# The four score products of an attention section take their banks together

## The chip, the cores and the metric

The kernel runs on one core of one Trainium2 chip. The metric is the device time of one execution in microseconds (us), the median of three runs. The core has five engines with a program each: TensorE (PE in the profile, with its weight loads as PEld), VectorE (DVE), ScalarE (ACT), GpSimd (POOL) and SyncE (SP). They meet at semaphores only.

## What is computed

A decoder of four layers with twelve sections (three kinds of attention, a delta rule, a state space section, dense and expert feed-forward sections) over 32 sequences of 128 tokens with 128 features. The change lies in the attention sections with 16 heads of 8 features, of which there are four. This is the one without a mask, cut to what matters:

```python
def _L0_xattn_ref(q, k, v, Wq, Wk, Wv, Wo):
    N_HEADS = 16
    query = split_heads(q @ Wq.T)
    key_ = split_heads(k @ Wk.T)
    value = split_heads(v @ Wv.T)
    scores = jnp.einsum('bhqd,bhkd->bhqk', query, key_) / jnp.sqrt(...)
    attn_probs = jax.nn.softmax(scores, axis=-1)
    attn_out = jnp.einsum('bhqk,bhkd->bhqd', attn_probs, value)
    return attn_out.transpose(0, 2, 1, 3).reshape(B, S, D_MODEL) @ Wo.T

x = x + _L0_xattn_ref(_layernorm(x, axis=-1), ctx_1024, ctx_1024, ...)
```

The other three (`L1_attn`, `L2_attn`, `L2_cross`) add a causal or a given mask to the scores before the softmax.

## The kernel before

Two streams (`STREAMS = 2`, called 0 and 1) of `G = 2` sequences each run interleaved. A round takes both through all twelve sections, and there are eight rounds; stream 1 starts six sections on, so that different sections of the two streams meet, and a first part brings stream 1 to that place. Inside a round each engine runs its own fixed list: the program of a stream is a Python generator for each engine, cut at its `yield`s, and the strings `TURNS` say for each engine which stream's next piece comes. Nothing reorders the lists afterwards. A "w" in the string of PE is a small product that nobody reads (`warm`, L2354).

Partial sums lie in eight PSUM banks. Two (`ACC`, one for each stream) are kept for accumulations, the other six form a ring that both streams share (`class Psum`). `open` gives the next bank of the ring and, on PE, emits a wait until the reader of the bank's last contents has given it back (semaphore `bank{b}_emptied`, incremented by `give`). `close` marks it filled; `take` is the reader's wait for that.

`attention16` is the code of the four sections. In it, for each sequence s of the two:

- `products(s, "S", ...)` (called by `scores`) makes the scores of 16 heads as four products, j = 0 to 3 (L728). Each contracts 32 rows (partitions 32j to 32j+31, so that each lies in its own quarter of TensorE's rows), has 512 columns in float32, and writes one bank. A float32 product is two MATMUL instructions in the profile, so four products are eight.
- With a mask, four more products (L698 causal, L701 given) add it, and only these close the banks. Without one (`L0_cross`, named x0) each product closes its own bank.
- DVE takes the negated maximum of each bank (`maxima`, L874) and gives the bank back; four short steps (L878 to L881) split the maxima into parts (`mparts`), which PE transposes (L747).
- `products(s, "T", ...)` makes the same scores transposed, again four products at L728. The subtraction of the maxima (L762) is added on PE, which closes the banks, and ACT takes the exponentials (L838, called from the piece behind L830). `values` (L778) multiplies with the values, `divide` (L886, L887) on DVE normalises.

The order of pieces on PE is: S of sequence 0, S of sequence 1, transposition and T of sequence 0, values and T of sequence 1, and so on. In x0 of stream 1 the other stream is in `L3_mamba`: on ACT L1622 to L1640, on DVE L1683 to L1713, on PE L1543 to L1577. Its preparation ends on DVE with L1687, which waits for ACT's L1628, and with L1692 to L1696, which wait for ACT's L1640; then 32 steps with a scan (L1707) each follow.

Of the kernel before, what the change touches and what calls it, by code (L numbers as in the profile page):

```python
# [25 lines left out]
B, L, D = 32, 128, 128  # L26
# [5 lines left out]
NJ, NI = 4, 4  # L32
# [286 lines left out]
def row_tiles(ap):  # L319

    return ap.rearrange("p (s f) -> p s f", f=128)
# [10 lines left out]
def build(nc, dram, out):  # L332
    with ExitStack() as st:
# [87 lines left out]
        def col(s):  # L421
            return slice(s * L, (s + 1) * L)
# [81 lines left out]
        def stream(u):  # L504
# [20 lines left out]
            def program(P, part):  # L525
# [149 lines left out]
                def attention16(nm, w, src=None, bias=False, bias_out=False, rope=False, mask=None):  # L675
# [29 lines left out]
                    def pe_f(pe):  # L705
# [6 lines left out]
                        for name, wn, s_ in todo:  # L712
                            t = P.open(pe, f"{nm}.{name}")
                            P.close(pe.matmul(t, W[w + wn][:], s_[:], start=True, stop=True), f"{nm}.{name}")
                        yield
                        t = P.open(pe, nm + ".v")
                        if bias:
                            bias_row(pe, t, W[w + "bv"][:])
                        for s in range(G):
                            last = pe.matmul(t[:, col(s)], src_ap[:, col(s)], W[w + "Wv"][:], start=not bias, stop=True,  # L720
                                             skip_group_check=True)
                        P.close(last, nm + ".v")

                        def products(s, letter, lhs, rhs):
                            for j in range(NJ):
                                r = slice(32 * j, 32 * j + 32)
                                t = P.open(pe, f"{nm}.{letter}{s}{j}", width=NI * L)
                                last = pe.matmul(row_tiles(t), lhs[r, col(s)], rhs[r, s], start=True,  # L728
                                                 stop=letter == "S" and mask is None, skip_group_check=True)
                                if letter == "S" and mask is None:  # L730
                                    P.close(last, f"{nm}.{letter}{s}{j}")

                        def scores(s):
                            yield
                            if s == 0 and not rope:
                                P.wait_given(pe, nm + ".q")
                            pe.wait_ge(ev(f"{u}.kz"), base["kz"] + s + 1)
                            products(s, "S", qk[0], kz)
                            if mask:
                                for j in range(NJ):  # L740
                                    P.close(masking(pe, P.bank(f"{nm}.S{s}{j}"), False, s), f"{nm}.S{s}{j}")

                        def turned(s):
                            yield
                            pe.wait_ge(ev(f"{u}.mparts"), base["mparts"] + s + 1)
                            t = P.open(pe, f"{nm}.mT{s}")
                            P.close(pe.transpose(t.bitcast(BF16)[:, 0:L], mparts[:, s, :], ident_bf[:]), f"{nm}.mT{s}")  # L747
                            yield
                            if s == 0:
                                pe.wait_ge(ev(f"{u}.qz"), base["qz"] + 1)  # L750
                            products(s, "T", qk[1], qz)
                            for j in range(NJ):
                                if j % 2 == 0 and j:
                                    yield
                                if mask:
                                    masking(pe, P.bank(f"{nm}.T{s}{j}"), True, s)
                                if j == 0:
                                    P.wait_given(pe, f"{nm}.mT{s}")
                                t = P.bank(f"{nm}.T{s}{j}")
                                for i in range(NI):  # L760
                                    a = NI * j + i
                                    last = pe.matmul(t[:, i * L:(i + 1) * L],  # L762
                                                     sel_part[:, a:a + 1].broadcast_to([128, 128]), mT[:, col(s)],
                                                     start=False, stop=i == NI - 1, skip_group_check=True)
                                P.close(last, f"{nm}.T{s}{j}")
# [26 lines left out]
                        t = P.open(pe, nm + ".y", ACC)  # L792
                        if bias_out:
                            bias_row(pe, t, W[w + "bo"][:])
                        for s in range(G):
                            yield
                            P.wait_given(pe, f"{nm}.O{s}")
                            last = pe.matmul(t[:, col(s)], oT[:, col(s)], W[w + "Wo"][:], start=not bias_out, stop=True,
                                             skip_group_check=True)
# [1625 lines left out]
        P = Psum(banks, filled, emptied)  # L2425
# [144 lines left out]
```

## Time and profile before

| what | value |
|---|---|
| median of three runs | 4992.15 us (4987.52 to 4992.7) |
| the profiled execution, its own time | 4994.97 us |
| its span, first to last instruction | 4993.3 us |
| mean granted clock of TensorE | 0.86 of full speed |
| PE / PEld / DVE / ACT / POOL busy | 82% / 57% / 65% / 41% / 13% |

The page of the profile gives busy time by engine, the span in 40 slices, and the costliest groups of instructions by line. The trace behind it can be asked for a stretch: the timeline lists instructions in order of time with the idle time of their engine before them and what released it, the list of waits sums such idle times by pairs, and the table of stretches gives busy time and granted clock (the PEclk column; 1.00 is 2.4 GHz, 0.50 is 1.2 GHz). The span without what lies around it is 1.7 us under the execution's own time.

### The profile page before, as it was taken

The numbers are of one execution on the slowest core, as the hardware profiler recorded it, in microseconds if no ns is written. First come the engines' busy times: TensorE is split into PE (matmuls) and PEld (weight loads), VectorE is DVE, ScalarE is ACT, GpSimd is POOL, SyncE is SP. The second block draws the span as 40 slices with busy tenths as digits, with TensorE's granted clock in tenths as the row PEclk, the third lists the DMA queues.
The fourth block names the chain that finished last, engine by engine and source line by source line (L and its number), as shares of the span: only waits on it lengthen the run. The fifth ranks groups of instructions, "written<-read, shape, count | busy, mean of one in ns | idle before, by whom it ended". The sixth has DMA issues, their size and how long they took to land. (4 is left out here: it accounts for less than half of the span.)

```text
span 4993.3 us, 97444 instructions
## 1 busy us (share of the span) xinstructions
PE 4078.1 (82%) x38655; PEld 2833.0 (57%) x38655; DVE 3236.5 (65%) x8464; ACT 2059.6 (41%) x4978; POOL 671.0 (13%) x1030
## 2 busy tenths in 40 slices
PE   2688888888888898888888888888888888888883
PEld 1455565656556566656556565555656565555652
DVE  3467767576766757676775767677675767677661
ACT  1245353534435353444435353443535344353530
POOL 1010201102010111101020110102011010102002
PEclk9689889798888889888888988898898988798897
DMA  4000000000000000000000000000000000000013
GB/s 125 1 2 1 7 1 7 1 3 5 1 7 1 6 2 7 2 1 7 1 7 1 6 2 6 2 1 7 1 7 1 4 4 1 7 1 6 2 33 89
DMA packets 70922, 46.81 MB, mean 9 GB/s; under 512 B 13095, under 2 KB 67488, under 8 KB 70226
## 3 DMA queue, kind: packets, MB, share of 16 engines
q1 hardware_dynamic: 65024, 33.82, 2.4%
q8 instruction: 322, 5.28, 0.4%
q0 software_dynamic: 2048, 3.85, 0.3%
q10 hardware_dynamic: 3378, 2.64, 0.2%
q14 instruction: 150, 1.23, 0.1%
HBM read 30.14 MB, written 10.50 MB: 8 GB/s over the span
## 5 line engine op out<-in xcount | busy, mean ns | idle before, releaser
L728 PE MATMUL banks<-scratch 32*128 32x512 f32 x2112 | 584.3, 764 | 74.8 <-ACT scratch L1635 36.2
L838 ACT ACTIVATE scratch<-banks 128x512 f32<-128x512 f32 x528 | 276.5, 600 | 254.6 <-PE banks L762 254.4
L301 ACT ACT_TABLE_LOAD x293 | 375.9, 1283 | 10.1 <-PE banks L1055 4.9
L874 DVE TENSOR_REDUCE scratch<-banks 128x4 f32<-128x512 f32 x528 | 330.0, 683 | 59.5 <-PE banks L728 36.1
L728 PEld LDWEIGHTS banks<-scratch 32*128 32x128 f32 x2112 | 205.3, 214 | 255.6 <-issue 84.8
L1650 ACT ACTIVATE scratch<-scratch,ssm_A 128x256 f32<-128x256 f32 x512 | 229.5, 500 | 264.5 <-DVE scratch L1707 251.9
L1562 PE MATMUL banks<-scratch,w_ident 128*128 128x256 f32 x1024 | 282.6, 399 | 57.0 <-DVE scratch L1713 56.9
L1707 DVE TENSOR_TENSOR_SCAN scratch<-scratch 128x512 f32<-128x512 f32 x256 | 313.2, 1224 | 12.6 <-ACT scratch L1650 5.2
L1846 PE MATMUL banks<-scratch 32*32 32x32 f32 (+1 forms) x11152 | 251.8, 206 | 48.8 <-issue 28.1
L1846 PEld LDWEIGHTS banks<-scratch 32*32 32x32 f32 (+1 forms) x11152 | 219.6, 119 | 101.9 <-issue 73.0
L1192 PE MATMUL banks<-experts,scratch 128*128 128x128 f32 x1792 | 261.3, 294 | 9.1 <-ACT scratch L1228 6.3
L1192 PEld LDWEIGHTS banks<-experts,scratch 128*128 128x128 f32 x1792 | 248.9, 207 | 30.2 <-issue 10.8
L1228 ACT ACTIVATE scratch<-banks,w_e_b 128x256 f32<-128x256 f32 x448 | 191.0, 472 | 174.7 <-PE banks L1184 173.2
L553 POOL TENSOR_TENSOR 1_rstd<-1_var,minus_half 128x2 f32<-128x2 f32 x102 | 75.5, 740 | 1354.8 <-DVE 1_var L571 1283.8
L1562 PEld LDWEIGHTS banks<-scratch,w_ident 128*128 128x128 f32 x1024 | 180.9, 195 | 105.9 <-DVE scratch L1713 87.8
L553 POOL TENSOR_TENSOR 0_rstd<-0_var,minus_half 128x2 f32<-128x2 f32 x96 | 67.1, 699 | 1190.5 <-DVE 0_var L571 1015.5
L886 DVE RECIPROCAL scratch<-banks 128x128 f32<-128x128 f32 x132 | 126.1, 955 | 151.9 <-PE banks L778 151.2
L778 PE MATMUL banks<-scratch 128*32 128x128 f32 x4224 | 220.5, 281 | 1.3 <-ACT scratch L838 1.3
L762 PEld LDWEIGHTS banks<-scratch,sel_part_bf 128*128 128x128 bf16 x2112 | 166.0, 105 | 95.6 <-issue 41.6
L2354 PE MATMUL banks<-ident_bf 128*128 128x256 bf16 x1128 | 175.6, 299 | 53.2 <-ACT scratch L824 21.7
L1701 DVE TENSOR_TENSOR scratch<-scratch,banks 128x512 f32<-128x512 f32 x256 | 174.5, 682 | 67.4 <-PE banks L1577 67.4
L778 PE MATMUL banks<-scratch,w_slots 128*32 128x128 f32 x4224 | 215.3, 276 | 0.0
(515 smaller groups left out, 8932.7 us busy)
## 6 DMA issues: line engine op xcount, KB each, us to landing
experts<-in_e_W SPq DMA_DIRECT2D x16, 256.0 KB, 5.4
w_e_W<-in_e_W SPq DMA_DIRECT2D x3, 704.0 KB
expert_in<-scratch SPq DMA_DIRECT2D x1, 2048.0 KB, 14.2
scratch<-expert_in SPq DMA_DIRECT2D x8, 256.0 KB, 4.6
expert_out<-scratch SPq DMA_DIRECT2D x8, 256.0 KB, 2.3
scratch<-residual SPq DMA_DIRECT2D x8, 256.0 KB
out<-scratch SPq DMA_DIRECT2D x8, 256.0 KB
experts<-in_e_w SPq DMA_DIRECT2D x1, 1792.0 KB, 7.8
```

What stands on the lines that cost most here:

```text
L301: act.preload_act_table_set(name)
L728: last = pe.matmul(row_tiles(t), lhs[r, col(s)], rhs[r, s], start=True, stop=letter == "S" and mask is None, skip_group_check=True)
L778: last = pe.matmul(t[32 * i:32 * i + 32, k * L:(k + 1) * L], W["slots"][:, 32 * j:32 * j + 32] if k else vslot[:, s, j, i, :], pT[:, s % 2 ...
L838: P.give(act.activation(pT[:, s % 2, j, :], t, ACT.Exp), f"{nm}.T{s}{j}")
L874: P.give(dve.tensor_reduce(negm[:, s, NI * j:NI * j + NI], row_tiles(t), X, ALU.max, negate=True), f"{nm}.S{s}{j}")
L1192: last = pe.matmul(t[:, col(s)], hid[:, e % RING, c, col(s)], w2[:, 2 * e + c, :], start=c == 0, stop=c == 1, skip_group_check=True)
L1228: P.give(act.activation(hid[:, e % RING, c, :], t, ACT.Gelu, bias=W["e2_b1"][:, 2 * e + c:2 * e + c + 1]), f"{nm}.u{e}.{c}")
L1562: last = pe.matmul(total[:, c * N:(c + 1) * N], ident[:], yc[:, k % RING, j, :], start=False, stop=n == DS - 2 and j == 1, skip_group_chec ...
L1650: ins = act.activation(decay[:, k % RING, j, :], dstart[:, c, :], ACT.Exp, scale=ssm_A[:, c, n + j:n + j + 1])
L1707: dve.tensor_tensor_scan(*flat, 0.0, ALU.mult, ALU.add).then_inc(ev(nm + ".state"), 1)
L1846: last = pe.matmul(t[dst, h * width:(h + 1) * width], lhs(h), rhs(h), start=True, stop=True, skip_group_check=True)
L2354: pe.matmul(banks[:, bank, 0:N].rearrange("p (s f) -> p s f", s=G), ident_bf[:], spread(ident_bf[:], G), start=True, stop=True, skip_group ...
```

## The change

The four banks of a group of four products are opened before the first product, in the same ring order. The waits that `open` emits therefore all stand in front of the product j = 0, and the products j = 1 to 3 wait for nothing. This holds for both letters, S and T, in all four sections. The turns, the banks of each name, the number of waits and the instructions of every engine stay as they are.

```diff
                         def products(s, letter, lhs, rhs):
+                            t = [P.open(pe, f"{nm}.{letter}{s}{j}", width=NI * L) for j in range(NJ)]
                             for j in range(NJ):
                                 r = slice(32 * j, 32 * j + 32)
-                                t = P.open(pe, f"{nm}.{letter}{s}{j}", width=NI * L)
-                                last = pe.matmul(row_tiles(t), lhs[r, col(s)], rhs[r, s], start=True,
+                                last = pe.matmul(row_tiles(t[j]), lhs[r, col(s)], rhs[r, s], start=True,
                                                  stop=letter == "S" and mask is None, skip_group_check=True)
```

On PE, in x0 of stream 1 within a round (S of sequence 0, S of sequence 1, the transposition, T of sequence 0), with each row's semaphores; `1.kz`, `1.qz` and `1.mparts` are operands that DVE and ACT prepare:

```order
-L728 MATMUL banks<-scratch 128x512 [waits bank5_emptied,1.kz,bank2_emptied]
-L728 MATMUL banks<-scratch 128x512 [waits bank0_emptied]
-L728 MATMUL banks<-scratch 128x512 [waits bank1_emptied]
-L728 MATMUL banks<-scratch 128x512 [waits bank2_emptied]
-L728 MATMUL banks<-scratch 128x512 [waits bank3_emptied,1.kz]
-L728 MATMUL banks<-scratch 128x512 [waits bank4_emptied]
-L728 MATMUL banks<-scratch 128x512 [waits bank5_emptied]
-L728 MATMUL banks<-scratch 128x512 [waits bank0_emptied]
+L728 MATMUL banks<-scratch 128x512 [waits bank0_emptied,bank1_emptied,bank5_emptied,bank2_emptied,1.kz]
+L728 MATMUL banks<-scratch 128x512 x3
+L728 MATMUL banks<-scratch 128x512 [waits bank5_emptied,bank4_emptied,bank0_emptied,bank3_emptied,1.kz]
+L728 MATMUL banks<-scratch 128x512 x3
```

No product has moved; the waits for banks 0 and 1 now stand ahead of the product into bank 5.

On DVE at the same place, the rows are the same before and after (`bank5_filled` says that the product j = 0 of sequence 0 has ended, `0s3.high` and `0s3.soft` come from ACT for the other stream):

```order
L874 TENSOR_REDUCE scratch<-banks 128x4 [waits bank5_filled,1.ones]
L1687 TENSOR_TENSOR scratch<-scratch 32x1024 [waits 0s3.high]
L874 TENSOR_REDUCE scratch<-banks 128x4 [waits bank0_filled,0s3.parts]
L874 TENSOR_REDUCE scratch<-banks 128x4 [waits bank1_filled]
L874 TENSOR_REDUCE scratch<-banks 128x4 [waits bank2_filled]
L878 CAST scratch<-scratch 128x16 [waits bank2_emptied]
L879 TENSOR_TENSOR scratch<-scratch 128x16 [waits dve_steps]
L880 CAST scratch<-scratch 128x16 [waits dve_steps]
L881 TENSOR_TENSOR scratch<-scratch 128x16 [waits dve_steps]
L1692 TENSOR_TENSOR scratch<-scratch 128x512 [waits 0s3.soft]
```

Nothing moved here; the first maximum stands ahead of L1687 in DVE's list.

## Rows read from the trace of the kernel before

**Rows 1.** The page, part 5: busy us, mean ns, idle before and releaser.

```profile
L728 PE MATMUL banks<-scratch 32*128 32x512 f32 x2112 | 584.3, 764 | 74.8 <-ACT scratch L1635 36.2
```

**Rows 2.** Timeline of PE, masked section: start us, length us, instructions [idle before <-releaser].

```profile
1622.00 1.14 PE L728 MATMUL banks<-scratch 32*128 32x512 f32 x8
1623.07 1.04 PE L698 MATMUL banks<-causal_bf,ident_bf 128*128 128x512 bf16 x4
1624.04 3.00 PE L728 MATMUL banks<-scratch 32*128 32x512 f32 x8
1626.97 1.04 PE L698 MATMUL banks<-causal_bf,ident_bf 128*128 128x512 bf16 x4
```

**Rows 3.** The same view at the half clock, a group that waits for no bank.

```profile
2031.84 2.09 PE L728 MATMUL banks<-scratch 32*128 32x512 f32 x8 [0.73 <-issue]
```

**Rows 4.** Who released L728's weight loads: us, times.

```profile
  DVE scratch L874: 85.8, 142
  ACT scratch L1635: 71.1, 40
```

**Rows 5.** Timeline of all engines, x0 of stream 1 in round 3.

```profile
1843.72 1.09 PE L728 MATMUL banks<-scratch 32*128 32x512 f32 x2 [0.84 <-issue]
1844.92 0.69 DVE L874 TENSOR_REDUCE scratch<-banks 128x4 f32<-128x512 f32 x1 [0.70 <-PE banks L728]
1846.97 1.22 DVE L1687 TENSOR_TENSOR scratch<-scratch 32x1024 bf16<-32x1024 f32 x1 [1.36 <-ACT scratch L1628]
1847.34 0.47 ACT L1635 ACTIVATE scratch<-banks,w_s_dt_b 128x256 f32<-128x256 f32 x1
1847.86 5.00 PE L728 MATMUL banks<-scratch 32*128 32x512 f32 x14 [3.05 <-ACT scratch L1635]
1848.05 0.48 ACT L1635 ACTIVATE scratch<-banks,w_s_dt_b 128x256 f32<-128x256 f32 x1
1848.58 0.62 PEld L728 LDWEIGHTS banks<-scratch 32*128 32x128 f32 x7 [0.23 <-ACT scratch L1635]
1850.04 1.94 DVE L874 TENSOR_REDUCE scratch<-banks 128x4 f32<-128x512 f32 x3 [1.85 <-PE banks L728]
1851.79 0.72 ACT L1640 ACTIVATE scratch<-scratch,ones_col 128x512 f32<-128x512 f32 x1
1852.64 0.17 DVE L881 TENSOR_TENSOR scratch<-scratch 128x16 bf16<-128x16 f32 x1
1852.74 0.69 DVE L1692 TENSOR_TENSOR scratch<-scratch 128x512 f32<-128x512 f32 x1
1852.87 0.10 PEld L747 LDWEIGHTS banks<-ident_bf,scratch 128*128 128x128 bf16 x1 [1.59 <-DVE scratch L881]
1854.65 1.70 ACT L1650 ACTIVATE scratch<-scratch,ssm_A 128x256 f32<-128x256 f32 x4 [0.84 <-DVE scratch L1696]
1855.27 1.69 PEld L728 LDWEIGHTS banks<-scratch 32*128 32x128 f32 x6 [1.68 <-DVE scratch L874]
1860.82 0.69 DVE L1701 TENSOR_TENSOR scratch<-scratch,banks 128x512 f32<-128x512 f32 x1 [2.98 <-PE banks L1577]
```

**Rows 6.** Who released DVE's L1687: us, times (all rounds).

```profile
  ACT scratch L1628: 10.9, 8
```

**Rows 7.** Table of stretches: length, busy us of PE, PEld, DVE, ACT, POOL, granted clock.

```profile
1840.40:1847.20 6.80, 3.56 (x14) 2.07 (x13) 2.85 (x6) 5.27 (x17) 0.00 (x0) 1.00 0.00 0
1847.20:1864.30 17.10, 16.32 (x81) 9.04 (x82) 11.68 (x24) 11.36 (x20) 0.00 (x0) 0.50 0.00 0
1864.30:1894.00 29.70, 26.35 (x247) 19.88 (x245) 27.95 (x41) 12.36 (x27) 0.70 (x1) 1.00 0.00 1
```

**Rows 8.** Timeline, x0 of stream 0: two releases of PE by ACT.

```profile
1559.61 0.47 ACT L1635 ACTIVATE scratch<-banks,w_s_dt_b 128x256 f32<-128x256 f32 x1
1560.19 0.29 PEld L728 LDWEIGHTS banks<-scratch 32*128 32x128 f32 x2 [2.47 <-issue]
1560.33 0.48 ACT L1635 ACTIVATE scratch<-banks,w_s_dt_b 128x256 f32<-128x256 f32 x1
1560.86 0.51 PEld L728 LDWEIGHTS banks<-scratch 32*128 32x128 f32 x6 [0.37 <-ACT scratch L1635]
1562.02 1.22 DVE L1687 TENSOR_TENSOR scratch<-scratch 32x1024 bf16<-32x1024 f32 x1
1563.27 0.69 DVE L874 TENSOR_REDUCE scratch<-banks 128x4 f32<-128x512 f32 x1
```

**Rows 9.** Cores: span and mean granted clock.

```profile
core 0: 4993.3 us, clock 0.860
```

## The prediction, made before the changed kernel ran

> **What bounds the kernel now.** I read the page's groups first, for the line that the diff touches, then the timeline around single groups of four products, then the list of releasers, and last one stretch on all engines. PE is busy 82% of the span, but busy time is no answer here. L728 stands in the page with 584.3 us of busy time [rows 1], in 2112 instructions, which are 264 groups of four products (2112/8). A group whose banks are all free takes 1.14 us at the full clock (the first row of [rows 2]) and 2.09 us at the half clock [rows 3]: the four products lie in four quarters of TensorE's rows and run side by side. A group whose banks come back one by one is longer, 3.00 us in [rows 2], because it starts piece by piece. What releases it is DVE's maxima (142 times) or ACT's L1635 (40 times) [rows 4]. So at these places the bound is the bank's reader, and PE waits with a product half way through its group.
>
> PE's list is strict at this point: between j = 0 and j = 3 nothing else stands in it. So the question is not what PE could do meanwhile, but who reads an early product before the last one has started.
>
> **With a mask, and for every T group: nobody.** The banks are closed by the masks (L698, L701) or by L762, which stand behind all four products. In [rows 2] the masks of the group of 1624.04 start at 1626.97, at the group's end. Whether j = 0 began at 1624.04 or with the last bank, the masks start at the same time, since the last product starts at the same time and takes as long alone as four do together: by the same rows the last one began no later than 1.14 us before the end. The early products were done early for no one.
>
> What is left there is the price of the waits themselves. Before, each product carries its own wait; now five waits stand in a row ahead of one. [Rows 8] have both: the product whose wait is one of several starts 0.11 us after ACT's end (1559.61+0.47 = 1560.08, start 1560.19), the one with a single wait 0.05 us after it (1560.33+0.48 = 1560.81, start 1560.86). So 0.06 us for each group that really waits for a bank. How many do? 182 releases of single products [rows 4], up to three in a group, so at least 60 groups, and at most all 264: 4 to 16 us. I take 100 groups, 6 us. For groups that find their banks free I take nothing, since PE's queue is worked through while earlier products still run. Below nothing this term can't go by this mechanism, as no wait is removed.
>
> **Without a mask (x0), S groups: DVE reads each product as it ends.** There are two such groups for each stream and round. In x0 of stream 0 the change costs little: sequence 1's first product starts at 1560.19, the others at 1560.86 [rows 8], and DVE, which has L1687 ahead of it until 1562.02+1.22 = 1563.24, takes the first maximum at 1563.27. Started at 1560.9 and 2.09 us long, the group would end at 1563.0, still before. L1687 is the cover here; without it this would cost up to 0.7 us a round.
>
> In x0 of stream 1 it is otherwise [rows 5]. The steps before:
> - the product j = 0 runs from 1843.72 to 1844.81, and DVE takes its maximum at 1844.92;
> - DVE then does L1687 of the other stream at 1846.97, which had waited 1.36 us for ACT;
> - j = 1 and j = 2 wait for the two banks that ACT's L1635 gives back at 1847.34+0.47 = 1847.81 and 1848.05+0.48 = 1848.53; j = 2 and 3 start at 1848.58;
> - DVE waits 1.85 us for j = 1 and takes the other three maxima from 1850.04 to 1851.98;
> - L878 to L881 end at 1852.81, PE's transposition starts at 1852.87, and L1692 starts at 1852.74, with its ACT operand there since 1851.79+0.72 = 1852.51.
>
> Afterwards all four wait for 1848.53. Queued behind that wait on PE are the rest of x0 and the other stream's products; queued on DVE behind the first maximum is L1687, which ACT had ready at 1846.94. Step by step: start at 1848.53 + 0.11 = 1848.64, or up to 0.1 later, as the wait for that bank is now the first of three steps; take 1848.7. The clock is the half one there [rows 7], so the group ends at 1848.7+2.09 = 1850.8. With the 0.11 us from a product's end to its maximum (1844.81 to 1844.92) the first maximum runs from 1850.9 to 1851.6, L1687 from 1851.6 to 1852.85, the other three maxima, 1.94 us, to 1854.8. Before, they ended at 1851.98. **This place costs 2.8 us a round**: 0.9 us because the first maximum now starts that much after the second one did before (1850.9 against 1850.04), and 1.9 us because a maximum (0.69) and L1687 (1.22), which DVE did while PE waited, now follow the wait. Bounds: 2.6 us if every hand-over is as short as the shortest seen, 3.1 us if the start comes 0.1 us later still and sequence 1's products, which before overlapped with sequence 0's (14 instructions in one run of 5.00 us) and now wait for a maximum of sequence 0, end after L881 and hold the transposition up.
>
> Is that on the path? I look for anything that does not move with it. ACT's next work, L1650, waited 0.84 us for DVE's L1696; PE's transposition waited 1.59 us for L881, and its T products 1.68 us for maxima; DVE's next pause (2.98 us at 1860.82) is for PE's L1577, which stands behind those T products in PE's list. So all three wait for the delayed chain, and POOL has nothing there. From 1864.3 on DVE is busy 27.95 of 29.70 us [rows 7] and can make up nothing. It happens in every round: L1687 waited for L1628 eight times, 10.9 us in all, 1.36 each [rows 6]. 8 x 2.8 = 22.4 us. The first part has only stream 1 and no L1687: nothing.
>
> **The sum.** 22.4 + 6 = 28.4 us. Against the profiled execution: 4994.97 + 28.4 = 5023.4 us, of which the span is 1.7 us less. That execution lies 2.8 us above the median, so against the median: 4992.15 + 28.4 = 5020.5, rounded to 5020 us. By the bounds of its terms the case reaches from 4992 + 8 x 2.6 + 4 = 5017 to 4992 + 8 x 3.1 + 16 = 5033.
>
> **A page on the packing.** The rows say that four free products take 1.14 us together and a spread group 3.00 us. The Trainium skill, "TensorE: Matmul & The Clock Gate", Part 3 on packing small matmuls, says that products in distinct row groups run concurrently, and gives 3.07 times for four tiles of 32 rows and 512 columns; it speaks for issuing the four together. By it, if the spreading were PE's own work, the change would bring L728 down to 264 x 1.14 = 301 us, and the 283 us of difference would be on offer. The trace agrees on the concurrency and not on the offer: the spread is waiting, by [rows 4]. It is the first half of rival C below.
>
> **Rivals.**
>
> A, *the delay is absorbed* (no change). If some branch that I took to move with the chain did not, for instance a table load of ACT or a later wait of DVE for a transfer, the 22.4 us shrink and the waits' 6 us stay: 4992 + 6 + perhaps a quarter of 22.4 = 5003 at most, 4995 to 5002 in the middle. For it: DVE is busy only 65% of the span, so there is slack somewhere. Against it: at 1852 to 1861 all three engines wait for the same chain [rows 5].
>
> B, *the clock falls longer*. In the stretch from 1847.2 to 1864.3 PE has the half clock [rows 7], after a wait in which it ran only one product; now it will run none, and the stretch begins 5 us before and ends 3 us later. Around the 60 to 100 masked groups too, PE's work is pushed together behind longer pauses. 17.1 us at half clock a round with PE's work growing by 3 us there costs 1.5 us a round, and as much again elsewhere: 8 x 3 = 24 us more, 5044.
>
> C, *faster*. The mechanism is the clock again, at the masked groups: the same work in denser pieces could bring the full clock sooner. Mean clock 0.860 [rows 9] means 28% of the span at the half clock (0.5 x 0.28 = 0.14), 1398 us. PE at its limit gains half a us for each us that comes back. It decides from 28.4/0.5 = 57 us returned (4% of 1398) for a tie, and for 0.2% faster from 77 us, which gives 4982; with 100 us it is 4970. Nothing in the rows shows such a return at a spread group, and PE waits at many places, so half a us is the most. The packing offer of the page, at the 4715 us that it would give (4992 + 6 - 283), I hold at 1 in 100.
>
> D, *nothing happens*: the lists of PE are the same except for the waits, so were the bank of j = 3 always free last and DVE never early, the time would be 4992. [Rows 5] rule this out at one place, and I put it with A.
>
> **How the numbers follow.** The likeliest is the sum, 5020, with 0.64. A and D together have 0.17, B has 0.12, C 0.07 (0.01 of it the packing). The range has to reach A's middle and B: I leave out C, the lowest of A and half of B, which comes to 4997 to 5041. A measurement of this kernel can tell 0.2% from no change, 10 us here, so faster is below 4982, slower above 5002. The forecast and B are slower (0.76), and of A a small part, against a small part of the forecast that falls short: slower 0.77. C is faster, but only in part by 10 us: 0.05. The rest, 0.18, is within 0.2%.
>
> **What would show it.** Right: in x0 of stream 1 of each round one run of L728 with nothing before 1848.6 (counted as here), DVE's first maximum, L1687 and three maxima in one piece behind it, no wait of L1687 for L1628 any more, and 2.6 to 3.1 us more from L865's start to L1692's. L728's busy time near 301 us at full clock and some 330 to 350 with the groups at half clock, while its idle time grows by as much. Masked groups 1.14 or 2.09 us long, their masks at the same distance from the last release plus 0.06. Wrong: the eight places each 2.8 us later but the rounds not longer (A), or a mean clock off 0.860 by more than 0.005, which is 50 us more or less at the half clock and up to 25 us of time (B, C).

## The result, and the profile after

| | before | after |
|---|---|---|
| median of four runs | 4992.42 us (4987.52 to 4996.94) | 5046.00 us (5032.10 to 5051.35) |
| ratio, 95% interval | | 1.0103 (1.0081 to 1.0126) |
| span of the profiled execution | 4993.3 us | 5049.7 us |
| its mean granted clock | 0.860 | 0.855 |

The change makes the kernel 1.0% slower, some 52 us. Forecast were 5020 us and a range up to 5041. The sign was right, the size was not. One of the runs of the kernel before that the experiments below are held against took 10744.17 us, at a mean clock of 0.404; it was far off all others, why is not known, and no ratio uses it.

Two rows of the page after, on the products and on the maxima (busy us, mean ns, idle before and its releaser), answer to [rows 1]. The third row is the one on the maxima in the page before:

```profile
L728 PE MATMUL banks<-scratch 32*128 32x512 f32 x2112 | 381.3, 791 | 306.0 <-DVE scratch L874 176.2
L874 DVE TENSOR_REDUCE scratch<-banks 128x4 f32<-128x512 f32 x528 | 329.3, 682 | 100.6 <-PE banks L728 72.5
```

```profile
L874 DVE TENSOR_REDUCE scratch<-banks 128x4 f32<-128x512 f32 x528 | 330.0, 683 | 59.5 <-PE banks L728 36.1
```

The products look cheaper by 203 us of busy time, and have 231 us more of idle time before them. That is not speed: a spread group's time was counted as busy from its first product on. What did get longer is DVE's wait for products, 72.5 us where it was 36.1, and that can cost time.

Now the place that carried the forecast, x0 of stream 1 in round 3, on all engines (timeline of after: start us, length us, engine, line; it answers to [rows 5]):

```profile
1857.36 0.48 ACT L1635 ACTIVATE scratch<-banks,w_s_dt_b 128x256 f32<-128x256 f32 x1
...
1858.09 2.09 PE L728 MATMUL banks<-scratch 32*128 32x512 f32 x8 [5.92 <-ACT scratch L1635]
...
1860.24 0.69 DVE L874 TENSOR_REDUCE scratch<-banks 128x4 f32<-128x512 f32 x1 [6.73 <-PE banks L728]
1860.96 1.22 DVE L1687 TENSOR_TENSOR scratch<-scratch 32x1024 bf16<-32x1024 f32 x1
...
1862.21 1.88 DVE L874 TENSOR_REDUCE scratch<-banks 128x4 f32<-128x512 f32 x3
...
1863.05 2.09 PE L728 MATMUL banks<-scratch 32*128 32x512 f32 x8 [2.87 <-DVE scratch L874]
...
1864.76 0.17 DVE L881 TENSOR_TENSOR scratch<-scratch 128x16 bf16<-128x16 f32 x1
1864.85 0.68 DVE L1692 TENSOR_TENSOR scratch<-scratch 128x512 f32<-128x512 f32 x1
...
1865.07 0.29 PE L747 MATMUL banks<-ident_bf,scratch 128*128 128x128 bf16 x1
```

No early product; DVE's first maximum, L1687 and the other three maxima in one piece behind the wait. From the end of ACT's L1635 (1857.84) to L1692 it is 7.01 us; before it was 4.21 (1848.53 to 1852.74). That is 2.8 us more, as forecast.

The other difference lies where the forecast had put almost nothing. T of sequence 0 in L1_attn of stream 0 (a causal mask; the forecast took such a group to cost 0.06 us), PE alone. First before, then after, round 3:

```profile
1628.79 1.03 PE L1562 MATMUL banks<-scratch,w_ident 128*128 128x256 f32 x4
1629.74 1.73 PE L728 MATMUL banks<-scratch 32*128 32x512 f32 x6
1631.78 1.12 PE L728 MATMUL banks<-scratch 32*128 32x512 f32 x2 [0.31 <-DVE scratch L1701]
1632.83 0.39 PE L698 MATMUL banks<-causal_T_bf,ident_bf 128*128 128x512 bf16 x1
...
1633.72 0.93 PE L2354 MATMUL banks<-ident_bf 128*128 128x256 bf16 x7
```

```profile
1637.62 1.03 PE L1562 MATMUL banks<-scratch,w_ident 128*128 128x256 f32 x4
1640.70 2.09 PE L728 MATMUL banks<-scratch 32*128 32x512 f32 x8 [2.06 <-DVE scratch L1701]
1642.72 0.61 PE L698 MATMUL banks<-causal_T_bf,ident_bf 128*128 128x512 bf16 x1
...
1644.13 0.93 PE L2354 MATMUL banks<-ident_bf 128*128 128x256 bf16 x7
```

The last bank comes from DVE's L1701 in both. From the product released by it to L2354 it was 1.94 us (1631.78 to 1633.72) and is 3.43 us (1640.70 to 1644.13). The steps are the same ones, at another clock. The table of stretches shows it (stretch and its length, busy time of PE, PEld, DVE, ACT and POOL, granted clock, share of DMA, GB/s), first before, then after:

```profile
1615.10:1649.30 34.20, 29.59 (x280) 18.11 (x278) 23.98 (x52) 10.30 (x30) 1.42 (x2) 1.00 0.00 1
```

```profile
1623.30:1640.40 17.10, 12.65 (x72) 7.29 (x70) 15.83 (x29) 5.51 (x20) 0.00 (x0) 1.00 0.00 1
1640.40:1643.80 3.40, 3.10 (x14) 1.25 (x15) 2.07 (x3) 0.01 (x1) 0.00 (x0) 0.50 0.00 0
1643.80:1660.90 17.10, 13.54 (x203) 9.84 (x201) 7.18 (x22) 5.27 (x11) 1.73 (x3) 1.00 0.00 1
```

Before, PE had 2.4 GHz there throughout. After, it fell to 1.2 GHz just as the group started, behind 2.06 us in which PE did nothing, where it had run three of the four products before. This is so in 6 of 8 rounds, and before in none. In the other two rounds of after PE had fallen to 1.2 GHz some 5 us before the group and was back at 2.4 GHz when it started, so in no round was this stretch spared.

To see where else time went I lined DVE's list of one kernel up with that of another, instruction by instruction, and compared the time between the same two instructions, mean of eight rounds. Below, "the steps" are these means. For after they say: 2.6 us a round more at x0 of stream 1, 1.3 at T of L1_attn. Some 20 us behind the latter it is 0.9 us less, since the next fall of the clock lasts 3.4 us there in most rounds, where it lasted 6.8 before. A third place shows 0.8 us more, at T of sequence 0 in L2_cross of stream 1, where the group ends at half clock in 8 of 8 rounds, before in 5. Some other steps differ by about 1 us in nearly every kernel that was compared with this profile of before, changed or not, so I take them for the draw of that one execution's clock.

### The profile page after: what moved, and what is told of

The parts are those of the page before. It is cut to its first block and busy times, and to the rows that moved or that the text cites. A ratio compares the mean times of both kernels' runs of the same rounds, so it can differ in the third digit from the quotient of the medians.

```text
span 5049.7 us, 97816 instructions
## 1 busy us (share of the span) xinstructions
PE 3881.7 (77%) x38655; PEld 2740.3 (54%) x38655; DVE 3233.6 (64%) x8464; ACT 2061.4 (41%) x4978; POOL 671.8 (13%) x1030
## 5 line engine op out<-in xcount | busy, mean ns | idle before, releaser
L728 PE MATMUL banks<-scratch 32*128 32x512 f32 x2112 | 381.3, 791 | 306.0 <-DVE scratch L874 176.2
L874 DVE TENSOR_REDUCE scratch<-banks 128x4 f32<-128x512 f32 x528 | 329.3, 682 | 100.6 <-PE banks L728 72.5
L728 PEld LDWEIGHTS banks<-scratch 32*128 32x128 f32 x2112 | 105.7, 220 | 386.4 <-issue 367.4
L1192 PEld LDWEIGHTS banks<-experts,scratch 128*128 128x128 f32 x1792 | 259.5, 215 | 26.6 <-ACT scratch L1228 9.7
L1701 DVE TENSOR_TENSOR scratch<-scratch,banks 128x512 f32<-128x512 f32 x256 | 174.1, 680 | 71.9 <-PE banks L1577 71.9
L2354 PE MATMUL banks<-ident_bf 128*128 128x256 bf16 x1128 | 175.2, 298 | 54.2 <-ACT scratch L824 21.7
L762 PE MATMUL banks<-scratch,sel_part_bf 128*128 128x128 bf16 x2112 | 209.5, 236 | 5.2 <-ACT scratch L830 5.2
```

The costliest lines, as they stand in the source:

```text
L728: last = pe.matmul(row_tiles(t[j]), lhs[r, col(s)], rhs[r, s], start=True, stop=letter == "S" and mask is None, skip_group_check=True)
L762: last = pe.matmul(t[:, i * L:(i + 1) * L], sel_part[:, a:a + 1].broadcast_to([128, 128]), mT[:, col(s)], start=False, stop=i == NI - 1, s ...
L874: P.give(dve.tensor_reduce(negm[:, s, NI * j:NI * j + NI], row_tiles(t), X, ALU.max, negate=True), f"{nm}.S{s}{j}")
L1192: last = pe.matmul(t[:, col(s)], hid[:, e % RING, c, col(s)], w2[:, 2 * e + c, :], start=c == 0, stop=c == 1, skip_group_check=True)
```

## The experiments

Each has the diff against the kernel before, in `products`. Where a line reads `together = ...`, the banks are opened together only where it holds:

```diff
+                            together = <condition>
+                            ts = [P.open(pe, f"{nm}.{letter}{s}{j}", width=NI * L) for j in range(NJ)] if together else None
                             for j in range(NJ):
                                 r = slice(32 * j, 32 * j + 32)
-                                t = P.open(pe, f"{nm}.{letter}{s}{j}", width=NI * L)
+                                t = ts[j] if together else P.open(pe, f"{nm}.{letter}{s}{j}", width=NI * L)
```

The added lines shift the numbers: L728 is L730 or L735 there, L874 is L876 or L881. Ratios are against the kernel before on the same chip in the same hour (medians 4980.98 to 4989.39 us; 22 to 35 runs), intervals are 95%. The ratio is not the quotient of the two medians: mostly they agree within 0.1 points, at e3 the quotient is 1.0040, at e12 1.0028.

### Which groups carry the loss

```diff
+ e1_x0_scores: together = letter == "S" and mask is None and not rope      (rope is off wherever mask is None)
```

> Only the S groups of the section without a mask (x0), of both streams, wait for all four banks; all other groups as before. Theory M (the maxima of DVE and L1687 come behind the wait in x0 of stream 1): about 20 to 23 us over the kernel before, +0.4 to 0.46%, with DVE's first maximum of that place near its last ones in each of the eight rounds. Theory K (most of the 54 us comes through TensorE's clock at the groups with masks and the T groups): the rest of the changed kernel's loss, some 30 us, is absent here. If the whole loss comes from x0, this kernel is 50 us slower.

Measured: 5010.43 us, ratio 1.0047 (1.0024 to 1.0070).

```diff
+ e2_all_but: together = not (letter == "S" and mask is None)
```

> The complement: every group waits for all four banks except the S groups of x0, which are as before. Theory K: 25 to 32 us over the kernel before (+0.5 to 0.65%), and a mean granted clock near 0.855 against 0.860. My recorded sum, which holds only 0.06 us for each group that waits: 4 to 16 us, clock unchanged. If x0 is the whole of it: nothing.

Measured: 5020.43 us, ratio 1.0081 (1.0050 to 1.0112), mean granted clock of its runs 0.857 against 0.863 before. That is 40 us, more than the 25 to 32 expected by the clock.

```diff
+ e3_one_place: together = letter == "S" and mask is None and u == 1 and s == 0 and part == "round"
```

> One group of each round only: S of sequence 0 in x0 of stream 1 waits for all four banks, eight times in the kernel. Theory M: 8 x 2.5 = 20 us (+0.4%), all of what e1_x0_scores costs within 5 us. If the overlap of sequence 1's first product with sequence 0's, which this kernel keeps, was worth something: up to 8 x 0.3 us less than e1_x0_scores.

Measured: 5004.35 us, ratio 1.0051 (1.0029 to 1.0074). The steps show +2.6 us a round at the place, nothing of it comes back in the 20 us behind it, and no other step grows by more than the draw. (The profiled execution is the fastest of the twelve, 4977.01 us at a clock of 0.869: the draw elsewhere hides the loss in its total, not in its steps.)

```diff
+ e4_turned: together = letter == "T"
```

> Only the T groups (of all four sections) wait for all four banks; the S groups as before. Theory K puts the one place that shows in all rounds of the changed kernel but one (T of sequence 0 in L1_attn of stream 0, 1.2 us later at the half clock) here: 10 to 20 us over before (+0.2 to 0.4%), and that group at the half clock (2.09 us long) in at least five of eight rounds, where the kernel before had it at the full one in all eight. Theory W (it is only the wait steps): under 5 us.

Measured: 5019.43 us, ratio 1.0078 (1.0050 to 1.0105), twice what was expected.

So the one place of x0, eight groups of 256 in the rounds, costs what all S groups of x0 cost, 0.5%, which is 25 us with an interval of 14 to 37 (the medians differ by 20); the forecast had 22.4. The rest of the change, forecast at 6 us, costs 0.8%, and the T groups alone cost as much. The two halves e1 and e2 add up to 1.28% against the 1.03% of the whole; the intervals allow both a plain sum and a smaller one.

### One T group, and the clock by itself

```diff
+ e5_one_turned: together = nm == "0a1" and letter == "T" and s == 0 and part == "round"
```

> One group of each round only: T of sequence 0 in L1_attn of stream 0 waits for all four banks. In the changed kernel PE idles 2.06 us before this group and has the half clock for it, and DVE's next wait for PE ends 1.3 us later on the mean of eight rounds. Theory K: 8 x 1.3 = 10 us over before (+0.2%), the group 2.09 us long in five or more of the eight rounds. Theory W (only the wait steps): 8 x 0.08 = 0.6 us, and the group 1.12 to 1.14 us long after its last bank in all rounds.

Measured: 4987.35 us, ratio 1.0022 (1.0005 to 1.0039). The group runs at half clock in 6 of 8 rounds, and the steps there are 1.5 us longer. As in after, part of it comes back: the steps some 20 us behind are 1.0 us shorter (e6, below: 0.3), with the next fall of the clock shorter. So of the 1.5 us about 0.7 a round, 6 us in all, are lost for good; the interval of the ratio reaches from 2 to 19 us. The timeline of PE and the stretches of e5 in round 3:

```profile
1623.57 1.03 PE L1569 MATMUL banks<-scratch,w_ident 128*128 128x256 f32 x4
1626.66 2.09 PE L735 MATMUL banks<-scratch 32*128 32x512 f32 x8 [2.06 <-DVE scratch L1708]
1628.68 0.61 PE L698 MATMUL banks<-causal_T_bf,ident_bf 128*128 128x512 bf16 x1
```

```profile
1609.50:1626.40 16.90, 14.18 (x70) 7.88 (x68) 15.89 (x29) 5.51 (x20) 0.00 (x0) 1.00 0.01 1
1626.50:1629.80 3.30, 3.14 (x14) 1.25 (x15) 1.92 (x3) 0.05 (x1) 0.00 (x0) 0.50 0.00 0
```

The same with work for PE during its wait, in a bank that it already has. Nobody reads it, and the product j = 0 overwrites it:

```diff
+ e6_one_turned_fill: as e5, and after the first bank is opened, three times:
+   pe.matmul(row_tiles(ts[0]), ident_bf[:], spread(ident_bf[:], NI), start=True, stop=True, ...)
```

> As e5_one_turned, and while it waits for the other three banks PE multiplies the identity by itself three times into the bank of j = 0 (3 x 512 columns, bfloat16, all 128 rows), which the product then overwrites. Theory K: the half clock at this group is gone (1.14 us in all eight rounds), DVE's next wait for PE is within 0.2 us of the kernel before, and the total is within 5 us of before. Theory W: no better than e5_one_turned, and 8 x 0.1 us worse if the filling stands in the way.

Measured: 4983.72 us, ratio 0.9996 (0.9982 to 1.0011). The group is at full clock in 8 of 8 rounds and the steps are back (+0.1 us). The intervals of e5 and e6 overlap, so the times alone do not tell them apart; the rows do. PE of e6 at the same place, then its stretch:

```profile
1627.70 0.81 PE L730 MATMUL banks<-ident_bf 128*128 128x512 bf16 x3
1629.92 1.14 PE L735 MATMUL banks<-scratch 32*128 32x512 f32 x8 [1.41 <-DVE scratch L1708]
1630.99 0.39 PE L698 MATMUL banks<-causal_T_bf,ident_bf 128*128 128x512 bf16 x1
```

```profile
1612.70:1646.60 33.90, 28.55 (x284) 17.99 (x282) 23.95 (x50) 10.02 (x29) 0.98 (x2) 1.00 0.00 1
```

The group waits for the same release and starts no sooner after it. All that e6 adds is 0.81 us of work ahead of it, and 2.09 us become 1.14. The loss at this place is the clock and not the wait.

### The other parts, and the waits by themselves

```diff
+ e9_turned_x0: together = letter == "T" and mask is None
```

> Only the T groups of x0 (both sequences, both streams) wait for all four banks. So far: T groups in all cost 0.78%, of which the one group of e5_one_turned is 0.22%; 0.56%, 28 us, is open. In e4_turned the stretch behind T of x0 in stream 1 is 1.0 us a round later and four of eight of its second groups have the half clock. Theory K: 8 to 16 us over before (+0.15 to 0.3%), with those second groups (T of sequence 1) at the half clock in some rounds. Theory W: 1 to 2 us.

Measured: 4995.79 us, ratio 1.0004 (0.9990 to 1.0018).

```diff
+ e10_turned_rest: together = letter == "T" and mask is not None and not (nm == "0a1" and s == 0)
```

> Only the T groups of the three masked sections wait for all four banks, without the one of e5_one_turned. If the costs add up, this and e9_turned_x0 come to 28 us together: 12 to 20 us over before here. Theory K wants single places with the half clock that the kernel before has not; theory W wants 0.06 to 0.1 us at each waiting group and no place above 0.3 us a round, 2 to 6 us in all.

Measured: 5007.74 us, ratio 1.0029 (1.0013 to 1.0045).

```diff
+ e11_masked_scores: together = letter == "S" and mask is not None
```

> Only the S groups of the masked sections wait for all four banks. From e2_all_but (0.81%) less e4_turned (0.78%): 0 to 5 us over before, within 0.25% in any case. If the parts do not add up because they compete for the same slack, up to 15 us.

Measured: 4989.48 us, ratio 1.0003 (0.9987 to 1.0018).

```diff
+ e12_wait_step: banks one by one as before; ahead of the fourth product of each group one more wait,
+   for a value that was reached before the group began (the operand kz or qz)
```

> The kernel before, with one more wait ahead of the fourth product of every group, for a semaphore that has its value already. The fourth product's start after its bank's release then takes the two steps that the trace shows elsewhere (0.105 us against 0.042), and nothing waits together. Theory W measured by itself: 0.063 us at some 20 groups a round, all of it on the path at most: 10 us over before (+0.2%); if about half is covered, 5 us. The clock stays at before's.

Measured: 5003.15 us, ratio 1.0007 (0.9992 to 1.0023). Its median lies 0.28% above that of before, more than the ratio over all runs says, so I take 0.3% as the bound.

By the clock, e9 was to cost 8 to 16 us, and nothing is measured there. For e10 it had 12 to 20 us at single places, which came out (0.29%, 14 us). An extra wait in each of 264 groups costs no more than 0.3%, with 0.07% the likeliest. The masked S groups, 96 of the 256, wait for all their banks and cost nothing that can be measured. The T parts add up to 0.55% (0.22, 0.04 and 0.29), inside the interval of e4 (0.50 to 1.05%) but at its lower end.

e10's loss starts at one place: in its steps, one is 1.6 us a round longer, at T of sequence 0 in L2_attn of stream 1. A second, 1.2 us, lies some 40 us behind it, at T of sequence 0 in L2_cross of the same stream, which ends at half clock in 8 of 8 rounds (before in 5). In 7 of 8 rounds the first group runs at half clock; in e4 it does in 2, in before and in after in none. PE of e10 in round 3, and its stretches:

```profile
1429.03 0.23 PE L749 MATMUL banks<-ident_bf,scratch 128*128 128x128 bf16 x1
1430.91 2.09 PE L730 MATMUL banks<-scratch 32*128 32x512 f32 x8 [1.66 <-DVE scratch L876]
1432.93 0.61 PE L698 MATMUL banks<-causal_T_bf,ident_bf 128*128 128x512 bf16 x1
```

```profile
1420.60:1430.70 10.10, 8.65 (x39) 4.37 (x37) 9.12 (x23) 6.41 (x20) 0.00 (x0) 1.00 0.00 0
1430.80:1434.10 3.30, 3.19 (x14) 1.25 (x15) 3.16 (x10) 0.16 (x2) 0.00 (x0) 0.50 0.00 0
```

In after the same group waits the same 1.65 us and then runs at full clock in all eight rounds. So the same wait costs 1 us or nothing. Even rounds of one kernel differ (e4: 2 of 8), with the same list of instructions; what decides between them was not isolated. To test this place alone:

```diff
+ e13_rest_fill: as e10, and the three filling products of e6 in the T group of sequence 0 of "1a2"
```

> The masked groups of letter T together except that of sequence 0 in L1_attn of stream 0, as in the run before that lost 0.29%, and at one of them (T of sequence 0 in L2_attn of stream 1, which there waits 1.66 us with nothing running and then runs at the half clock in 7 of 8 rounds) three filling products of 128 rows x 512 columns that nobody reads, while PE waits. Clock theory: the loss sits at that one place (DVE's steps there came 1.6 us later a round, 8 x 1.6 = 13 us of 14), so it goes: 4990 to 4996 us, within 0.1% of before; the group 1.14 us in 8 of 8 rounds. Rival, the loss is spread over all groups as longer waits: 0.2 to 0.35% remain.

Measured: 4989.58 us, ratio 1.0007 (0.9994 to 1.0019). The group is at full clock in 8 of 8 rounds and the step is back (-0.1 us), and so is the second step behind it (-0.1 us), though nothing was filled there. Three products at one group of eight rounds give back what e10 lost.

### Filling everywhere

If filling gives back the clock at one place, it might everywhere.

```diff
+ e7_after_fill: together = True; three filling products in each T group of sequence 0
+   and in each S group of sequence 1 that has a mask
+ e8_all_but_fill: the same, but S of x0 one by one as before
```

> The whole change, with the same three filling products in every T group of sequence 0 and every masked S group of sequence 1. Theory K: the clock's share of the loss (25 to 30 us) goes, the 20 us of x0 in stream 1 stay: +15 to +25 us over before (+0.3 to 0.5%), mean clock 0.862 or more. Theory W: still 45 to 55 us over before.

Measured: 5083.98 us, ratio 1.0212 (1.0187 to 1.0238).

> As e7_after_fill, with the S groups of x0 as in the kernel before. Theory K: no slower than before, and perhaps faster, since PE is busier in its waits than it was with one or two early products: -30 to +5 us. Theory W: 25 to 40 us over before, like e2_all_but.

Measured: 5055.12 us, ratio 1.0149 (1.0126 to 1.0171).

Both expectations missed, by far. The filling did its work at T of L1_attn (+0.1 us in the steps, as in e6), but mean clock did not rise (0.854), and other steps grew by 1.0 to 2.6 us. Where the banks were free there was no wait to fill, as in this stretch of PE in e7:

```profile
1777.38 0.82 PE L730 MATMUL banks<-ident_bf 128*128 128x512 bf16 x3
1778.13 1.14 PE L735 MATMUL banks<-scratch 32*128 32x512 f32 x8
```

The group follows with no idle time, so the 0.8 us stood in its way. Of the 14 filled groups of a round five had waited 0.43 us or less in after, too little to hold the filling. How much of the 1.1% more than the plain change came from such places and how much from the clock falling elsewhere was not separated.

### The two places back

```diff
+ e14_two_back: together everywhere, except T of sequence 0 of "0a1",
+   and S of sequence 0 of x0 in stream 1, both in the rounds
```

> The whole change except at two places of a round, where the banks are opened one by one as before: S of sequence 0 in x0 of stream 1, and T of sequence 0 in L1_attn of stream 0. Theory, the two places carry the larger part (0.51% and 0.22% alone): 0.2 to 0.5% slower than before remain, 0.5 to 0.8% less than the whole change's loss. Rival, everything loses a little at each of 256 groups: 0.9% or more remains. Rival, the loss comes wherever the clock next falls, so that taking one place away only moves it: 0.6 to 0.9%.

Measured: 5011.55 us, ratio 1.0045 (1.0029 to 1.0060). Of the 1.03%, 0.58 points are gone with 16 of 264 groups; the two alone had cost 0.51 and 0.22. The remaining 0.45% lies in no single place. No score group waiting in x0 of stream 1 adds to it: from its first maximum to the end of its T groups the steps are those of before within 0.1 us, though S of sequence 1 still waits for all its banks. T of L2_attn is at full clock in this kernel; the step at T of L2_cross of stream 1 is 0.6 us longer, with half clock in 6 of 8 rounds. The rest are steps of 0.2 to 0.8 us, no larger than the draw of the clock between two executions. That part stays open.

### Filling in the kernel before

In before, 17 us at half clock begin in x0 of stream 1 [rows 7]. Does filling help there, with no change of the waits?

```diff
                                 t = P.open(pe, f"{nm}.{letter}{s}{j}", width=NI * L)
+                                for _ in range(5 if j == 0 and <place> else 0):
+                                    pe.matmul(row_tiles(t), ident_bf[:], spread(ident_bf[:], NI), start=True, stop=True, ...)
+ e15_fill_x0: <place> is S of sequence 0 in x0 of stream 1; e16_fill_x0_both: that and T of sequence 0
```

> The kernel before, and five filling products (128 rows x 512 columns, nobody reads them) ahead of the first score product of sequence 0 in x0 of stream 1, in its own bank. In the profile of before 17 us at the half clock begin there in each round. Filling lengthens the way to DVE's first maximum by 1.1 us, against 1.36 us that DVE waits for ACT behind it. Theory, the clock follows the work done before it: the group behind runs in 1.14 us in place of 2.09, 0.5 to 1 us a round, 4 to 8 us faster (0.1 to 0.15%). Rival, the clock there falls whatever the filling, since the groups behind are spread: no change or up to 4 us slower.

Measured: 4991.36 us, ratio 1.0007 (0.9990 to 1.0025).

> The same with five filling products also ahead of the other groups of sequence 0 in x0 of stream 1 (letter T). Clock theory: that group and the steps behind it come at the full clock, up to 2 us a round more: 8 to 20 us faster than before. Rival: filling stands in PE's list after the wait and adds 1.1 us a round to the path, 5 to 9 us slower, as filling in every group did.

Measured: 4985.59 us, ratio 0.9995 (0.9982 to 1.0008).

The clock answered: the group of S is at full clock to its end in 4 of 8 rounds of each kernel, and in one more (e15) or two more (e16) the clock falls only inside its last product, where before it ran at half clock in all eight, and the mean clock of e16's runs is 0.867 against 0.861. That is some 60 us less at half clock, and the time did not move. Rows of e15 in round 3 show why (timeline, all engines; L1695 is L1692 of before, L1643 its L1640):

```profile
1843.17 3.81 PE L731 MATMUL banks<-scratch 32*128 32x512 f32 x14 [1.86 <-ACT scratch L1638]
...
1844.40 1.95 DVE L877 TENSOR_REDUCE scratch<-banks 128x4 f32<-128x512 f32 x3 [0.90 <-PE banks L731]
...
1847.10 0.72 ACT L1643 ACTIVATE scratch<-scratch,ones_col 128x512 f32<-128x512 f32 x1
...
1847.86 0.69 DVE L1695 TENSOR_TENSOR scratch<-scratch 128x512 f32<-128x512 f32 x1 [0.68 <-ACT scratch L1643]
```

DVE waits 0.90 us for the maxima's bank in place of 1.85 [rows 5], and then 0.68 us for ACT. Of the 0.95 us gained only 0.27 come through; the rest is a new wait. DVE waits there for ACT in 5 of 8 rounds of e15 and 6 of 8 of e16 (0.1 to 0.7 us), and before in none. So no kernel here beats the one before.

## Why the prediction was right, and where it was wrong

**The place of x0: right, in its size too.** Forecast 2.8 us a round, 22.4 us; the rows show 2.80 in round 3, the steps 2.6 in the mean, and e3, which changes only this, 25 us (14 to 37). Its parts: the group started 0.25 us after the release (1857.84 to 1858.09) where I took 0.17; the first maximum 0.06 us after the group's end where I took 0.11. L1687 waits for L1628 no more: L1687's idle time is 0.5 us in all, where the waits for L1628 alone were 10.9 [rows 6]. The upper bound's reason hardly bit: sequence 1's products end 0.2 us after L881, and the transposition starts 0.14 us after it, where before it was 0.06. That the delay would not be absorbed (rival A) was right: in the steps of e3 all of it is still there 20 us on.

**x0 of stream 0 and the first part: nothing, right.** All S groups of x0 (1.0047) cost no more than the one place (1.0051).

**The masked and T groups: wrong.** This is the step that failed: "Whether j = 0 began at 1624.04 or with the last bank, the masks start at the same time, since the last product starts at the same time and takes as long alone as four do together". It is true at one clock, and the clock was taken as given. The early products were read by no one, and yet they did something: they kept TensorE at work during the wait. Without them the last product runs, in some groups, at 1.2 GHz, and with it the masks that DVE and ACT wait for. For these groups the sum had 6 us; e4 alone has 39 us (25 to 52). Of the term itself, 0.06 us for a wait in a row of several, nothing was wrong that the runs can tell: e12 bounds it at 0.3% and the 96 masked S groups cost 0.03% (-0.13 to 0.18). Its count was read wrongly: the numbers of [rows 4] are idle times of weight loads and of products together, so the 182 releases count some products twice (157 are of weight loads, 25 of products). Counted by weight loads alone at least 52 groups wait, not 60, which changes the term little.

**Rival B was the mechanism, and I held it at 0.12.** It gave 5044 us, and 5046 was measured, but that agreement is partly luck. B placed half of its 24 us inside the x0 stretch, where the runs show nothing above the forecast, and called the other half "as much again elsewhere" without looking for a place. [Rows 2] had the candidates in plain sight: groups that PE spreads over 3 us of waiting. The question that I did not ask at each of them was what PE will have run in the microseconds before the group, once the early products are gone.

**Rival C's first half.** The Trainium skill, "TensorE: Matmul & The Clock Gate", Part 3 (packing small matmuls), says that products in distinct row groups run concurrently, which speaks for issuing them together. Here L728's busy time did fall by 203 us, three quarters of the 283 us on offer by it, and none of that came back as time: what [rows 4] said, that the spread is waiting, was right.

**What I said would show it.** L728's busy time was to be 330 to 350 us, which is 31 to 52 groups at half clock ((330 - 301)/0.95 to (350 - 301)/0.95). It is 381, 85 groups by the same sum. Already before, 69 of the 256 groups in the rounds have half clock in their last product, wholly or in part; I had taken the rows of two full-clock groups for most. After it is 83. A mean clock off by more than 0.005 was to be the sign of B or C; it is off by 0.0052 in the profiled runs (0.8603 to 0.8551), and I had written down what it would mean: up to 25 us.

**What stays open.** The one place of x0 (0.5%) and the T groups (0.55% as the sum of parts, 0.78% together) cover the loss of 1.03% (0.81 to 1.26); simply added they come to 1.1 or 1.3%, and the intervals do not say whether they add. Inside the T groups two places were isolated with a run that loses and one that fills (e5 and e6, e10 and e13). The second of them is at full clock in after, so in the change itself it is not that place that costs. That the rest of the T groups' loss is the clock too was not tested by a run. What remains there behind the two places put back, 0.45% (0.29 to 0.60), is not found.

## What to carry to other kernels

Before you merge waits, ask of each early product two things: who reads it before the last one starts, and what the engine will have done in the wait without it. The first is seen in the readers' queue (and in what is queued behind the reader's first step); the second only in the granted clock of the stretch, and there a wait of 2 us with nothing in it can make the next steps 1.5 us longer, of which a part may come back behind. Filling such a wait with work that nobody reads gave this back at the two places where it was tried alone, and filling by rule made the kernel slower, at least where there was no wait to fill. So fill by place.

## What the hardware showed that I had not expected

- A wait of 2.06 us with nothing running was followed by 1.2 GHz at once (e5, 6 of the 7 rounds that had this wait), and 0.81 us of bfloat16 products on all 128 rows inside that wait kept 2.4 GHz (e6, 8 of 8). The neighbouring group, S of sequence 1, waits 1.90 us in after (1634.85 in its trace) and stays at full clock in 6 of 8 rounds; in the other two the clock falls inside it, and these are the two in which the T group behind it is spared.
- A fall can be partly paid back: with the one at T of L1_attn (e5) the next one, some 20 us on, lasted 3.4 us in 7 of 8 rounds, where in before it lasted 6.8 in all eight. The steps were 1.5 us longer, then 1.0 shorter.
- The same group with the same 1.65 us of wait was at half clock in 7 of 8 rounds of one kernel (e10) and in none of another (after). A kernel's loss by the clock can't be read from a wait's length alone.
- Time at half clock has no fixed price. The profiled execution of after has some 68 us more of it than that of before (2 x (1 - 0.8551) x 5049.7 against 2 x (1 - 0.8603) x 4993.3), and after loses; e16 has some 60 us less and gains nothing, and the steps that it speeds up end, in 6 of 8 rounds, in a wait for ACT.
- The mean clock of one and the same kernel drew between 0.855 and 0.873 over its 24 runs of the first series, and its time over 43 us (4958.89 to 5002.18). With 12 runs and more of each kernel the intervals were still 0.25 to 0.46 points wide, so effects of 0.2% could be told only beside the steps of the trace.
